# A graph-attention kernel whose first two gating chunks are also split between row gathers and TensorE picks, with half of the expert units placed behind the chunk loop

## The reference, cut to what matters

```python
h = (x_flat @ W_gat).reshape(M, HEADS, NUM_EXPERTS)
a_src = (h * att_src).sum(-1)
a_dst = (h * att_dst).sum(-1)
e = jax.nn.leaky_relu(a_src[src] + a_dst[dst], negative_slope=0.2)
e_max = jax.ops.segment_max(e, dst, num_segments=M)
ee = jnp.exp(e - e_max[dst])
denom = jax.ops.segment_sum(ee, dst, num_segments=M)
alpha = ee / (denom[dst] + 1e-16)
msg = h[src] * alpha[:, :, None]
agg = jax.ops.segment_sum(msg, dst, num_segments=M).reshape(M, HEADS * NUM_EXPERTS) + b_gat
scores = _layernorm(agg, ln_gamma, ln_beta).reshape(M, HEADS, NUM_EXPERTS).mean(1)
topk_s, topk_i = jax.lax.top_k(scores, TOP_K)
w = jax.nn.softmax(topk_s, axis=-1)
for ei in range(NUM_EXPERTS):
    g = jnp.where(topk_i == ei, w, 0.0).sum(-1)
    hh = jax.nn.gelu(x @ W1[ei] + b1[ei], approximate=False)
    out = out + g[..., None] * (hh @ W2[ei] + b2[ei])
```

## Time and profile before

| | |
|---|---|
| median of 3 runs | 2878.49 us (2878.16 to 2880.92) |
| the profiled execution: its own time / its span | 2875.96 us / 2873.8 us |
| busy: PE, DVE, ACT, POOL | 41%, 70%, 19%, 64% |
| gathers from `d_h` | 668 indirect DMAs |
| pick matmuls (L990) | 10080 (15 chunks x 672) |
| expert matmuls, L963 and L951 | 128 and 512 records |

### The profile page before, as it was taken

The page is one execution under the profiler, slowest core; times in us unless marked ns, Lnnn a source line. Parts: engine busy times, 40 slices in busy tenths (PEclk is TensorE's granted clock), DMA queues, the critical chain, the costliest instruction groups (busy, mean ns, idle before and its releaser), DMA issues.

```text
span 2873.8 us, 33943 instructions
## 1 busy us (share of the span) xinstructions
PE 1188.8 (41%) x12474; PEld 993.0 (35%) x12474; DVE 2000.9 (70%) x3060; ACT 550.8 (19%) x633; POOL 1839.1 (64%) x1768
## 2 busy tenths in 40 slices
PE   4854000000000100001135968888888897830515
PEld 3422000000000000001023535878888897830315
DVE  7788686888778778778974011888888888840536
ACT  1010001222232222122010112222222222220301
POOL 0000677777777777774776777777777777757062
PEclk9967555555555555555555555999999999975557
DMA  9400312333233333332127271121221212111011
GB/s 307 150 0 3 81 42 78 101 114 111 81 111 97 96 112 96 98 94 61 31 86 36 29 151 22 24 37 24 34 26 24 38 23 37 24 39 14 1 13 34
DMA packets 156178, 185.36 MB, mean 64 GB/s; under 512 B 94692, under 2 KB 114854, under 8 KB 150038
## 3 DMA queue, kind: packets, MB, share of 16 engines
q1 hardware_dynamic: 99602, 120.23, 14.0%
q0 software_dynamic: 56352, 62.34, 13.4%
HBM read 96.24 MB, written 86.23 MB: 63 GB/s over the span
## 4 chain that ended last, share of the span: by engine, by line
POOL 53%; issue 21%; DVE 13%; PE 7%; DMA 2%; ACT 2%; SPq 1%; POOLq 0%; DVEq 0%; ACTq 0%
POOL arena L671 50%; DVE arena L1282 8%; PE psum L872 2%; POOL d_adseed L754 2%; POOL d_qseed L695 1%; PE psum L951 1%; DVE arena L1285 1%; PE psum L963 1%; PE psum L788 1%; SPq L507 1%; PE psum L990 1%; PE psum L1049 1%; DVE psum L1557 0%; ACT arena L1127 0%; DVE arena L1578 0%
## 5 line engine op out<-in xcount | busy, mean ns | idle before, releaser
L1282 DVE TENSOR_TENSOR arena<-arena 128x512 f32<-128x512 f32 (+17 forms) x1331 | 870.4, 694 | 231.2 <-ACT arena L1091 60.6
L671 POOL DMA_INDIRECT arena<-d_h,arena x668 | 693.7, 1038 | 206.4 <-issue 206.1
L671 POOL DMA_INDIRECT arena<-in_kv,arena x640 | 645.3, 1008 | 200.1 <-issue 194.4
L990 PE MATMUL psum<-arena 128*128 128x128 bf16 x10080 | 616.3, 224 | 87.7 <-DVEq L1772 80.0
L990 PEld LDWEIGHTS psum<-arena 128*128 128x128 bf16 x10080 | 601.4, 101 | 94.1 <-DVE arena L1285 80.9
L788 PE MATMUL psum<-arena 128*128 128x128 f32 (+4 forms) x568 | 116.0, 375 | 1228.5 <-DVEq L1357 1038.3
L788 PEld LDWEIGHTS psum<-arena 128*128 128x128 f32 (+4 forms) x568 | 91.7, 198 | 1254.2 <-DVEq L1357 1053.3
L1285 DVE TENSOR_SCALAR arena<-arena 128x512 bf16<-128x512 f16 (+8 forms) x1054 | 339.2, 380 | 76.2 <-ACT arena L1183 19.4
L1282 DVE TENSOR_TENSOR arena<-psum,arena 128x512 f32<-128x512 f32 (+1 forms) x177 | 166.6, 949 | 207.3 <-PE psum L951 200.5
L671 POOL DMA_INDIRECT arena<-d_adst,arena x40 | 54.3, 1358 | 303.6 <-DVEq L1454 291.7
L1557 DVE TENSOR_TENSOR_SCAN psum<-psum,arena 128x1024 f32<-128x1024 f32 x40 | 91.9, 2298 | 135.7 <-ACT arena L1114 134.7
(11 more groups left out here) (156 smaller groups left out, 1357.2 us busy)
## 6 DMA issues: line engine op xcount, KB each, us to landing
d_gs<-arena SPq DMA_DIRECT2D x32, 768.0 KB, 14.6
d_as<-arena SPq DMA_DIRECT2D x20, 1152.0 KB, 4.5
d_qseed<-arena SPq DMA_DIRECT2D x5, 4096.0 KB, 29.6
arena<-d_qseed SPq DMA_DIRECT2D x20, 1024.0 KB, 6.0
arena<-d_h,arena POOLq DMA_INDIRECT x668
arena<-in_kv,arena POOLq DMA_INDIRECT x640
d_adseed<-arena SPq DMA_DIRECT2D x1, 4096.0 KB, 29.6
arena<-d_adseed SPq DMA_DIRECT2D x17, 128.0 KB
```

What stands on the lines that cost most here:

```text
L671: return pool.indirect_dma_start(out, None, table, bass.IndirectOffsetOnAxis(index[:, t:t + 1], 0))
L990: last = nc.tensor.matmul(ps[2 + turn_of(b, m)][:, k * PICK_W:(k + 1) * PICK_W], pick_hot[turn_of(b, m)][:, t, k * P:(k + 1) * P], h_split ...
L1282: return V.tensor_tensor(o, a_, b_, op)
```

## The change

- Chunks 0 and 1 gather 36 columns each, as all others, and pick 28. `g_gather` loses its row count, and the semaphore arithmetic (`HS_EACH`, `chunk_count`, `pick_keys_set`) is shifted to count from chunk 0.
- Ahead of the loop stand 8 expert groups (32 units) and not 14. The picks of chunks 0 and 1 follow them on PE, ACT and DVE, written out ahead of the loop. `flags`, `maximum` and `weighted_sums` of chunk 0 go into the picks of chunk 1, in the places that the loop gives them.
- Behind the loop stand 8 groups (32 units) and not 2, where the two were.

```diff
-        HS_FIRST, HS_EACH = 16 * (G_RUN + 1), 16 * (G_RUN - PICKS + 1)
-        EXPERTS_FIRST, EXPERTS_EARLY = 10, 14
+        HS_EACH = 16 * (G_RUN - PICKS + 1)
+        EXPERTS_EARLY = 8
...
-            def g_gather(b, n_rows):
+            def g_gather(b):
                 gather_rows(ad_first[b], d_ad, g_fidx[b], 0).then_inc(hs_in[b], 16)
-                for j in range(n_rows):
+                for j in range(G_RUN - PICKS):
                     gather_rows(hs[b][:, j, :], d_h, g_sidx[b], j).then_inc(hs_in[b], 16)
             for b in range(2):
                 pool.wait_ge(g_idx_in[b], 48)
-                g_gather(b, G_RUN)
+                g_gather(b)
...
-            with pe.If(n_all >= 3):
-                for m in range(2):
+            for m in range(2):
+                spread(0, 0, m)
+            for m in range(BATCHES - 2):
+                spread(0, 0, m + 2)
+                pick(0, 0, m)
+            for m in range(2):
+                pick(0, 0, BATCHES - 2 + m)
+                spread(0, 1, m)
+            for m in range(BATCHES - 2):
+                spread(0, 1, m + 2)
+                pick(0, 1, m)
+            for m in range(2):
+                pick(0, 1, BATCHES - 2 + m)
+                with pe.If(n_all >= 3):
                     spread(1, 0, m)
...
             for n in range(4 * EXPERTS_EARLY):
                 gelu(n)
-                if n == 4 * EXPERTS_FIRST - 1:
-                    lay(0, 0, 0)
-                    weigh(0, 0, 0)
-                    rows(0, 0, 0)
...
+            for m in range(BATCHES):
+                all_keys(0, 0, m)
+            for m in range(2):
+                all_keys(0, 1, m)
+            all_keys(0, 1, 2)
+            all_keys(0, 1, 3)
+            lay(0, 0, 0)
+            all_keys(0, 1, 4)
+            weigh(0, 0, 0)
+            all_keys(0, 1, 5)
+            rows(0, 0, 0)
+            all_keys(0, 1, 6)
...
-            for grp in range(EXPERTS_FIRST):
+            for grp in range(EXPERTS_EARLY):
                 expert_group(grp)
...
-            flags(0, 0, 0)
-            maximum(0, 0, 0, True)
-            weighted_sums(0, 0, 0)
-            for grp in range(EXPERTS_FIRST, EXPERTS_EARLY):
-                expert_group(grp)
...
+            pick_keys(0, 0)
+            for m in range(2):
+                one_hot(0, 0, m)
+            for m in range(BATCHES - 2):
+                one_hot(0, 0, m + 2)
+                take_picked(0, 0, m)
+            pick_keys(0, 1)
+            for m in range(2):
+                one_hot(0, 1, m)
+                take_picked(0, 0, BATCHES - 2 + m)
+            picked_a_src(0, 0)
+            p_done[0] = 0
+            flags(0, 0, 0)
+            for m in range(BATCHES - 2):
+                one_hot(0, 1, m + 2)
+                take_picked(0, 1, m)
+                if m == 1:
+                    maximum(0, 0, 0, True)
+                if m == 2:
+                    weighted_sums(0, 0, 0)
+            for m in range(2):
+                with dve.If(n_all >= 3):
+                    if m == 0:
+                        pick_keys(1, 0)
+                    one_hot(1, 0, m)
+                take_picked(0, 1, BATCHES - 2 + m)
+            picked_a_src(0, 1)
```

More of the change, by code:

```diff
@@ L482, in chunk_count @@
         def chunk_count(it, b, per, n):
-            return it * (2 * per) + ((b - 2) * per + n)
+            return it * (2 * per) + (b * per + n)
         def turn_of(b, m):
@@ L773, in _ @@
                         pool.sem_inc(waits_carried, 1)
-                        g_gather(b, G_RUN - PICKS)
+                        g_gather(b)
             pool.wait_ge(g_stored, 3)
@@ L976, in spread @@
                 if m == 0:
-                    pe.wait_ge(pick_keys_set, it * 2 + (b - 1))
+                    pe.wait_ge(pick_keys_set, it * 2 + (b + 1))
                 pe.wait_ge(pick_all_set, chunk_count(it, b, BATCHES, m + 1))
@@ L1159, in lay @@
                 nc.scalar.copy(by_f[:, :, 1:], ad_seed[b].rearrange("p j f -> p f j")[:, :, 1:])
-                act.wait_ge(hs_in[b], it * HS_EACH + (HS_FIRST - HS_EACH * back * b))
+                act.wait_ge(hs_in[b], it * HS_EACH + (HS_EACH - HS_EACH * back * b))
                 nc.scalar.copy(by_f[:, :, 0], ad_first[b]).then_inc(g_laid, 1)
@@ L1789, in _ @@
             dve.sem_inc(pick_taken, 2)
-            with dve.If(n_all >= 3):
-                pick_keys(1, 0)
-                one_hot(1, 0, 0)
-                one_hot(1, 0, 1)
+            pick_keys(0, 0)
[25 more added lines that the diff above has]
+            picked_a_src(0, 1)
             with dve.Fori(1, G_CHUNKS // 2 + 1) as it:
```

## The result

The changed kernel takes **2938.16 us** (median of 4 runs, 2934.87 to 2945.29) beside 2878.32 for the kernel before in the same comparison: ratio 1.0211, 95% interval 1.0188 to 1.0234. The forecast was 2922, range 2900 to 2936. The direction was right; the size was 16 us too small and the time lies 2 us outside the range. The profiled execution took 2935.45 us with a span of 2933.3, so that the forecast's sum of 2919.6 missed by 15.9.

The account below looks back on a forecast made before the run. The prediction took POOL's issue of indirect DMAs as the bound until chunk 16's last gather. It summed 2875.96 - 50 + 93.6 = 2919.6, and with 2.5 for the median of runs forecast 2922 us, range 2900 to 2936.

Parts of the forecast that it names:

- Head: Ahead of the loop: 56 fewer POOL gathers start chunk 2 at 1751 instead of 1800.8 us, gaining 50 us.
- Tail: Behind the loop: six more expert groups at 15.60 us each, in series and uncovered, cost 93.6 us.
- The step that failed: In the loop: DVE and PE need 47.3 us a chunk, POOL 50.4, so POOL's old pace holds, 50 us earlier.
- The first: Behind the loop: units run at 2.4 GHz, 1.95 us each, total about 2870 us; chance 0.06.
- The second: Start of chunk 2: POOL is not held up, the full 73.8 us count, total 2898 us; chance 0.05.
- third: Ahead of the loop: picks run at 1.2 GHz, some 45 to 50 us more, total 2972 us; chance 0.04.
- The fourth: Tail partly covered or entry slower, for instance by code loading for written-out picks; 2930 to 2950 us; chance 0.07.

Follow-up runs that it names:

- the placed kernel: The changed kernel with padding ahead of PE's loop, so that its first instruction starts an instruction fetch block; 2926.12 us, ratio 1.0162.

## Why the forecast missed

- **Head.** Right, step by step: chunk 2 at 1751.43 (forecast 1751) behind 24.23 us of waiting (24), -49.4 against -50.
- **Tail.** Right: 93.8 and 94.7 in two kernels against 93.6. It was a price of the place as well as of the units, which the forecast didn't ask: with the eight groups behind the carries' store, some 27 us less passed from the tail copy to the end.
- **The step that failed** is "from landing to landing DVE and PE need 49.2 - 1.9 = 47.3 us, POOL 50.4, so the loop is POOL's again at its old pace". 47.3 came from one chunk, and that chunk had no back edge ahead of it. The scans of the kernel before give 47.8 for such a chunk and 51.8 for one that has the back edge (means of six), 99.56 for two. Against POOL's 100.8 that leaves 1.2 us an iteration, not the 6.2 of the forecast (100.8 - 2 x 47.3). A margin that thin did not survive the change of PE's code: with the second stop moved from 25 matmuls behind the back edge to 11, two chunks took 101.55, and PE and DVE became the bound.
- **The 15.8 us, term by term.** DVE's scan of chunk 1 is 41.8 us earlier (1785.42 against 1827.24) and POOL's chunk 2 is 49.4 earlier, so PE and DVE enter the loop 7.6 us later against POOL. From there to the scan of chunk 15 they need 711.0 us instead of 696.6, another 14.4. Against this stand 6.2 us of slack that the kernel before had in its last chunk (42.1 us from the scan of chunk 15 to the last one, with DVE waiting behind POOL's last gathers; 35.9 in the changed kernel). Even at the old pace 1.4 us would have been lost.
- The near tie was in the trace of before: the scans over the whole loop show it. Where the second stop would fall could not be read from it, so that some 14 us more should have been in the range: 7 iterations of 2 us.
- **Rivals.** The first (units behind the loop at 2.4 GHz) came for a moment: from 2640 to 2651 the changed kernel's PE was granted 1.00 and an L963 record took 1.12 us. Then it waited 13.24 us for DVE, and from 2664 to 2768 it was at 0.50, busy 103.82 of 104 us. DVE's first add came after the fast ones were done, so they gained nothing. The second and third did not occur. The fourth, a dearer entry by code loading, named something near the cause, the loading of code, but at the entry, where the picks came as forecast (first batch of chunk 1 at 1712.79, forecast 1712.3); it was in the loop; its 2930 to 2950 held the result at a chance of 0.07.
- The Trainium skill, page "Runtime: NRT & Kernel Launch", section "Instruction fetch mechanics", says that a taken branch out of the current window costs a fetch, while crossing from one block to the next is mostly hidden. The trace agrees on the first (2.8 to 3.2 us at each back edge) and not on the second, if the second stop is such a crossing: 1.5 to 2.0 us after 11 matmuls, none when the loop's head starts a block. That it is one is inferred from the placed kernel; no trace shows the fetches themselves.

## What to carry to other kernels

Take the pace of a loop from whole iterations, back edge included, and from many of them, on every engine; compare those paces before saying who bounds it, and treat a margin of 1% as a tie. Code changed ahead of a loop moves where the loop's instructions lie, and this alone cost 2 us an iteration here, so try a placed head for a large loop. Before moving work behind a loop, look for what is waited for there: the empty iterations and the order of units and carries were worth 106 us, more than the exchange itself.

## What the runs showed of the hardware

- **Long DVE instructions on SBUF hold POOL's indirect DMAs** until they end: a gather of 0.94 us took 8.71 beside a scan of 8.68 and ended 0.8 us behind it. Scans and `tensor_tensor` with both operands in SBUF do it, and the gather of 2.99 us lay beside a `tensor_scalar` of 2.28 us with one.
```profile
1885.33 2.40 POOL L671 DMA_INDIRECT arena<-d_h,arena  x1 [0.31 <-issue]
1888.03 2.68 POOL L671 DMA_INDIRECT arena<-d_h,arena  x1 [0.30 <-issue]
```

  Each of the kernel before's 16 earlier scans comes with two such gathers, together 54.8 us above 0.94 each. So about 3.4 of the 50.40 us that a chunk takes on POOL are DVE's doing, and the two engines' paces are not independent.
- **On two chips the engines stand idle in issue for long stretches**, as if their instructions came late. On them the kernel before took 3833 to 3853 us where it took 2876 to 2879 elsewhere. PE's timeline of the placed kernel there, in the middle of one batch:

```profile
2503.50 2.65 PE L990 MATMUL psum<-arena 128*128 128x128 bf16 x39
2507.21 0.28 PE L990 MATMUL psum<-arena 128*128 128x128 bf16 x2 [1.05 <-issue]
...
2533.40 0.27 PE L990 MATMUL psum<-arena 128*128 128x128 bf16 x1 [2.52 <-issue]
2536.90 0.26 PE L990 MATMUL psum<-arena 128*128 128x128 bf16 x1 [3.23 <-issue]
```

  Matmuls come one to three at a time, mostly 1.4 to 3.5 us apart, for some 50 us, then whole batches run at full pace again. Waits of PE at L990 for issue add up to 567.8 us there, and to 11.9 us in the changed kernel on the chip of the result. What is slow on these chips no run here shows.
